# Order of sums and products in the gated output stage, and the first loads requested from two engines

## What is computed

```
s1, s2 = cond[:, :256], cond[:, 256:]
# attention layers (two): x*s1 is normalised over its channels; q, k, v, w and u are projections,
# each scaled by rsqrt(square(weight) . square(style) + 1e-8)
x = x + attention(x)
# scan layers (two):
xr, gate = split(x @ W_in.T)
xn = layernorm(silu(conv4(xr + t_emb)))            # 512 channels
h  = clip(h * ad + bd * xn_t, -10, 10)             # for each token, 16 states x 512 channels
ys = sum over states of c * h
y  = ys + D * xn
x  = x + (y * silu(gate)) @ W_out.T
```

## Time and profile before

| | |
|---|---|
| median of 3 runs | 1805.43 us (1805.3, 1805.43, 1807.08) |
| profiled execution, its own time | 1802.89 us |
| span of its trace | 1801.1 us |
| mean granted TensorE clock | 0.983 |
| busy: PE, DVE, ACT, POOL | 94%, 90%, 73%, 38% |
| moved by DMA | 226.85 MB |

### The profile page before, as it was taken

How to read it: one execution, slowest core, us unless ns; L and a number is a source line. 1 busy time by engine, 2 the same in 40 slices (tenths; PEclk the granted TensorE clock), 3 DMA queues, 4 the chain that set the end, 5 groups by cost and what they waited for, 6 DMA issues and landing times.

```text
span 1801.1 us, 43797 instructions
## 1 busy us (share of the span) xinstructions
PE 1684.4 (94%) x14852; PEld 749.3 (42%) x14852; DVE 1629.7 (90%) x2492; ACT 1306.5 (73%) x2213; POOL 686.3 (38%) x702
## 2 busy tenths in 40 slices
PE   6999999999999999899999999999998999999998
PEld 3555555555554555332222224445553322222244
DVE  5899999999987999989999998679999999999976
ACT  5655556465646999889999992069998999999910
POOL 0223233232331332457676650002335576756400
PEclk9999999999999999799999999999998999999999
DMA  4000001000002344554555667624345445456677
GB/s 161 2 2 0 1 2 31 2 1 0 2 1 83 133 162 156 183 168 140 182 154 188 218 187 220 212 83 173 132 176 187 152 141 183 151 189 198 188 232 262
DMA packets 126312, 226.85 MB, mean 126 GB/s; under 512 B 35604, under 2 KB 61204, under 8 KB 117268
## 3 DMA queue, kind: packets, MB, share of 16 engines
q1 hardware_dynamic: 126200, 225.35, 38.2%
HBM read 141.95 MB, written 83.36 MB: 125 GB/s over the span
## 4 chain that ended last, share of the span: by engine, by line
PE 24%; ACT 19%; DVE 15%; issue 7%; DMA 3%; POOL 1%; DVEq 1%; ACTq 0%; SPq 0%; POOLq 0%
ACT R L1058 17%; PE PS L1173 5%; PE PS L1505 5%; PE PS L1522 5%; DVE q L2080 4%; DMA sgp<-sg_d 3%; PE PS L1571 2%; DVE acc L1762 2%; DVE z L1920 2%; PE PS L1365 2%; PE PS L1340 1%; PE PS L1382 1%; DVE yf L2116 1%; DVE xp L1758 1%; DVE z L1891 1%
## 5 line engine op out<-in xcount | busy, mean ns | idle before, releaser
L1058 ACT ACTIVATE R<-q,Ast 128x512 f32<-128x512 f32 x1016 | 633.0, 708 | 35.2 <-DVE q L2080 33.0
L2080 DVE SCALAR_TENSOR_TENSOR q<-R,PS 128x512 f32<-128x512 f32 x1008 | 610.9, 684 | 9.4 <-PE PS L1505 5.1
L629 POOL TENSOR_TENSOR Uw<-Ub,rowmask 96x512 bf16<-96x512 bf16 x256 | 335.6, 1344 | 145.4 <-PE PS L1505 133.3
L1505 PE MATMUL PS<-xq,Uw 97*128 97x512 bf16 x1024 | 329.3, 394 | 42.4 <-DVE q L2080 34.5
L1522 PE MATMUL PS<-q,Wy 128*32 128x512 f32 x2016 | 282.0, 615 | 0.4 <-DVE q L2080 0.4
L1505 PEld LDWEIGHTS PS<-xq,Uw 97*128 97x128 bf16 x1024 | 85.0, 97 | 362.0 <-DVE q L2080 270.8
L1173 PE MATMUL PS<-X,Win 128*128 (+1 forms) x456 | 213.9, 607 | 0.1
L1074 PE MATMUL PS<-xn,Wl 128*128 128x512 f32 x384 | 186.6, 610 | 0.8 <-DVE xn L1644 0.7
L550 POOL TENSOR_TENSOR ex<-ex,rs 128x1024 f32<-128x1024 f32 x32 | 76.8, 2400 | 164.2 <-DVE rs L1667 164.2
L1762 DVE SCALAR_TENSOR_TENSOR acc<-xp,Wc,acc 128x512 f32<-128x512 f32 x192 | 134.7, 752 | 2.6 <-DVE eC L1884 0.2
L543 POOL TENSOR_TENSOR vsc<-vTd,vs_t 128x1024 f32<-128x1024 f32 x16 | 41.6, 2600 | 217.9 <-ACT vTd L768 217.9
(11 more groups left out here) (183 smaller groups left out, 2622.7 us busy)
## 6 DMA issues: line engine op xcount, KB each, us to landing
xq<-xpart_d SPq DMA_DIRECT2D x384, 192.0 KB
sg_d<-sg SPq DMA_DIRECT2D x16, 1024.0 KB, 5.3
xn_d<-z SPq DMA_DIRECT2D x16, 1024.0 KB, 3.9
y_d<-ys SPq DMA_DIRECT2D x64, 256.0 KB, 3.9
xnp<-xn_d SPq DMA_DIRECT2D x16, 1024.0 KB, 8.0
sgp<-sg_d SPq DMA_DIRECT2D x16, 1024.0 KB, 11.6
xpart_d<-xh SPq DMA_DIRECT2D x16, 512.0 KB, 2.9
xpart_d<-xmi SPq DMA_DIRECT2D x16, 512.0 KB, 3.7
```

Source lines behind the costliest of these rows:

```text
L629: pl.tensor_tensor(Uw[0:XROWS, h, w, :, :, :], Ub[0:XROWS, w, 0:N, ds(s0, CH)].rearrange("p n t -> p t n").unsqueeze(2).broadcast_to([XROW ...
L1058: act.activation((end if end and (h, t) == (1, CH - 1) else R)[:, w, :], q[:, t % 2, w, :], ACT.Relu, scale=Ast[:, h, w, t:t + 1], bias=CL ...
L1505: pe.matmul(PS[:, w, :], Uw[0:KROWS, h, w, t, :, :].rearrange("p b n -> p (b n)"), xq[0:KROWS, hb, w, s8 % XT, :], start=True, stop=True). ...
L2080: v.scalar_tensor_tensor(out=q[:, s8 % 2, w, :], in0=R[:, w, :], scalar=2 * CLIP, in1=PS[:, w, :], op0=ALU.min, op1=ALU.subtract).then_inc ...
```

## The change

In `gated`, the four sums yf of a group are written first, in one loop, and the four products yg behind them, in a second one. A wait is added ahead of the first sum of each group but the very first: all products yg of the group before must be written, since they read yf.

At the start, X's group 0 and the weights Wl[0] are no longer requested by SP but by ACT, ahead of its first table load: X's group 0, then q and k (512 KB) with a semaphore of their own, then v, w and u (768 KB). ACT's squaring of q and k waits for the new semaphore, the other waits for Wl[0] stay with the old one, which now counts v, w and u.

```diff
+        w_qk_in = sem("att_weights0_qk")
...
         def _(sp):
             sp.dma_start(cond[:, :, :], condT).then_inc(cond_in, 16)
-            sp.dma_start(X[:, 0, :, :], xT[:, 0]).then_inc(x_in[0], 16)
             sp.dma_start(masks[:, :], masks_d).then_inc(spr_in, 16)
             sp.dma_start(spread[:, :, :], spread_d).then_inc(spr_in, 16)
-            sp.dma_start(Wl[0][:, :, :, :], attw[0]).then_inc(w_in[0], 16)
             sp.dma_start(X[:, 1, :, :], xT[:, 1]).then_inc(x_in[1], 16)
...
+            act.dma_start(X[:, 0, :, :], xT[:, 0]).then_inc(x_in[0], 16)
+            act.dma_start(Wl[0][:, 0:2, :, :], attw[0][:, 0:2]).then_inc(w_qk_in, 16)
+            act.dma_start(Wl[0][:, 2:5, :, :], attw[0][:, 2:5]).then_inc(w_in[0], 16)
             logarithm_set()
...
             def weight_squares(l, ws=range(5)):
-                act.wait_ge(w_in[l], 16)
+                if l == 0 and ws == range(2):
+                    act.wait_ge(w_qk_in, 16)
+                else:
+                    act.wait_ge(w_in[l], 16)
...
                 def gated(g):
                     it, u = l * G + g, g % 2
                     v.wait_ge(po_in[u], (l * (G // 2) + g // 2) * 32 + 32)
+                    if it:
+                        v.wait_ge(yg_r, it * DC)
                     for m in range(DC):
                         v.wait_ge(po_mm, it * DC + m + 1)
                         v.scalar_tensor_tensor(out=yf[:, m, :], in0=xnp[:, u, m, :], scalar=Dsk[:, m, :], in1=PS[:, m, :],
                                                op0=ALU.mult, op1=ALU.add).then_inc(yf_r, 1)
+                    for m in range(DC):
                         v.wait_ge(yf_r, it * DC + m + 1 + DC)
                         v.tensor_tensor(yg[:, u, m, :], yf[:, m, :], sgp[:, u, m, :], ALU.mult).then_inc(yg_r, 1)
```

## The result

| | before | changed |
|---|---|---|
| median | 1805.3 us (5 runs, 1800.24 to 1807.08) | 1791.3 us (5 runs, 1790.33 to 1793.67) |
| profiled execution, span | 1802.89, 1801.1 us | 1792.12, 1790.3 us |

The ratio is 0.9931, 95% interval 0.9914 to 0.9948: by it the change is 12 us faster (14.0 by the medians), where 7.4 were forecast. 1791.3 lies under the range's lower end of 1795.8.

A forecast was written before the change was run, and what follows sets the result against it. Loads of xnp, sgp and y were taken to pace the gated stages' middle, PE their end, Wl's landing the start. Terms -2.5 - 3.2 - 1.7 = -7.4 us from 1805.43 gave 1798.0 us, range 1795.8 to 1802.3.

The forecast's parts named there:

- the level: Whole kernel: the median of the runs shown, 1805.43 us, was the start from which the 7.4 us were subtracted.
- the middle stage's: Gated stage of the first of the last two layers: group 6's product starts sooner, -2.5 us, bounds -0.5 and -2.7.
- Pace of DVE: Gated stages, each group: sums start every 0.66 us, products every 0.61; fourth sum ends at 2.72, last product at 5.16.
- PE's queue: Gated stages: turn_y(g+1) stands before outward(g) and waits for the fourth sum; outward starts at 3.37 us, 2.07 sooner.
- Landings move with the first request: Gated stages: DMA engines are full until group 6 has its loads, so all landings move 0.46 us sooner.
- last: Gated stage of the last layer: group 6's product starts 3.8 or 2.7 us sooner; the middle, -3.2 us, was taken.
- Start: First loads: q and k land sooner, so ACT squares them sooner; -1.7 us, between gains of 0 and 2.5.
- the row-by-row end of the estimate: First loads: if engines take a row from each queue in turn, q and k land at 7.4 us, gain 2.5.
- The loads only sharing the bandwidth: Rival 2, start: Wl's first part lands at 11.3 us as before, at most 0.46 gained; 1799.7 us, chance 0.18.
- The stages set by the loads alone: Rival 3, gated stages: loads, not PE, set the end, each stage gives only 0.5 us; 1802.7 us, chance 0.15.
- The clock, the slower rival: Rival 4, last two products: PE's gathered waits drop the clock, 13.9 us become up to 27.8; 1811.9 us, chance 0.05.

The follow-up runs named there:

- e2: The kernel before with only the first loads changed (three requests on ACT), sums in the old order: 1797.84 us against 1800.35, ratio 0.9986.
- e3: The kernel before once more, without any edit, for a second profiled execution: ratio 0.9997, runs from 1794.4 to 1803.52 us.
- e4: The kernel before with Wl[0] cut in two transfers (q and k, then v, w and u), all requested by SP: 1798.26 us, ratio 0.9987.
- e1: The kernel before with only the order of sums and products changed, first loads still with SP: 1794.95 us against 1800.35, ratio 0.9968.
- e5: The changed kernel measured a second time, unedited, beside the kernel before: 1794.64 us against 1800.57, ratio 0.9976.
- e8: The kernel before with the new order of sums and Wl[0] cut in two on SP's queue, no requests moved to ACT: 1793.66 us, ratio 0.9966.
- e11: The changed kernel measured a third time, unedited, beside the kernel before: 1792.84 us against 1800.21, ratio 0.9955.
- e6: The kernel before (old order) without the loads of xnp and sgp for groups 2 to 7, output differs: 1794.61 us, ratio 0.9969.
- e7: New order of sums and products, without the loads of xnp and sgp for groups 2 to 7, against the kernel before: 1792.07 us, ratio 0.9958.
- e10: New order and split on SP, each stage's first gate load (group 2) requested behind group 1's products, against the kernel before: 1803.53 us, ratio 1.0020.

## Why the prediction was right or wrong

The landings and stages of all profiles with the gate loads requested alike, from each timeline, in us from the stage's first sum:

| | old order: before, e2, e3, e4 | new order: changed, e1, e5, e8, e11 (third run) |
|---|---|---|
| group 6's first sum, middle | 55.21, 53.20, 53.69, 56.00 (mean 54.5) | 52.21, 52.72, 53.42, 51.80, 50.86 (52.2) |
| group 6's first sum, last | 54.67, 57.05, 53.91, 53.77 (54.9) | 54.91, 54.94, 55.88, 55.02, 55.15 (55.2) |
| stage, middle | 81.46, 79.93, 80.16, 82.25 (81.0) | 76.49, 77.48, 77.70, 76.08, 75.98 (76.7) |
| stage, last | 75.30, 76.54, 73.30, 73.15 (74.6) | 72.33, 73.16, 74.26, 72.59, 73.95 (73.3) |

- **The step that failed is the level.** "The median of the runs shown is 2.5 us above it, so the forecast is 1805.43 - 7.4 = **1798.0 us**": this took three runs as the level from which to subtract. 78 later ones put the kernel before at 1800.2, which makes 5.2 of the 6.7 us by which 1791.3 lies under the forecast; from 1800.2 the same 7.4 give 1792.8, itself under the range. Of its width only 0.6 us, from 1805.4 - 9.0 = 1796.4 down to 1795.8, was left for what runs differ by. In the first set the kernel before stood 5.1 us above its later level and the changed kernel 1.5 to 3.3 under its own; why is open. The difference forecast, 7.4 us or 0.9959, is 0.0005 from the mean of the three measurements, lies inside the interval of the third, 0.0002 below the second's and 0.0011 above the first's.
- **The term that was mis-sized is the middle stage's,** -2.5 forecast with a bound of -2.7, -4.97 in the pair of profiles and -4.2 by the means below. The order on PE's queue gives 1.96 of it (e6 and e7); the rest came with group 6's landing, counted as 0.46 us sooner and 2.3 sooner in the means.
- **Pace of DVE, right.** 2.72 and 2.49 us, groups 0 and 1 5.22 us apart instead of 5.54. The Trainium skill, "VectorE: DVE Perf Modes", section "The DRAIN you can't avoid", says that a semaphore after each operation of a chain costs nothing extra; the prediction read that for the wait too. Read so it does not fit: a product that waits for its own sum starts 0.78 us behind it, an independent sum 0.66. Of the semaphore alone no run here tells, since both orders have one after every operation.
- **PE's queue, right.** Where PE waited for the sums of the changed kernel, the product came 3.38 to 3.41 us behind the first of them, 3.37 forecast. Without loads the stage gains 1.96 and 1.97 of 2.07 forecast.
- **Landings move with the first request: borne out for a late request, off in size for the sooner one.** The request was 0.49 us sooner (5.22 instead of 5.71 behind the first sum, 0.46 forecast) and e10 shows that a late first request makes all later landings late. That the engines have no hole behind it was argued and is borne out in part (group 3 of e10). But in the means the middle stage's landing moved by -2.3 and the last's by +0.3. The terms: middle stage -2.5 forecast and -4.2 by the means (above), last -3.2 forecast and -1.3; together -5.7 and -5.5, and e1 measured 5.8. In the last stage half of the difference between -3.8 and -2.7 was counted as gained from "8.57 instead of 7.03"; no other profile of the old order has a fall of the clock there, and three of five of the new order have one (last point). Why the landings of the two stages differ is open.
- **Start, -1.7 forecast, 2.06 in the pair of profiles, 1.9 by the means, 2.5 by e2's ratio.** The size was right, the way partly wrong. q and k landed at 6.4 us, before the 7.4 of the row-by-row end of the estimate, and what held the start was spread, a small transfer of the other queue, by which ACT's mean part was 0.54 us late. The prediction had it "go up to 0.9 us sooner"; it was requested 0.47 us sooner and landed 2.1 us later than before (8.7 against 6.6).
- **Rivals.** The loads only sharing the bandwidth: out for q and k, though its reason, the same DMA engines behind both queues, fits spread's coming late. The stages set by the loads alone, 0.5 us each: out, the means give 4.2 and 1.3, and by e6 and e7 the order pays without the loads. e10 shows that the loads set the pace up to group 6, as the prediction assumed. The clock, the slower rival: its mechanism is real, its size small. Between 1760 and 1770 us the clock fell in e1, e5 and the third run of the changed kernel (0.83 over 10 us in each), not in the changed kernel's own profile and e8, nor in e2, e3 and e4; the product of group 6 then came 4.28, 4.44 and 4.86 us behind its first sum, where the changed kernel's own profile has 3.41 and e8 3.64. That is 0.6 to 1.5 us, and the last two products ran at full speed every time (13.9 us). All five profiles of the new order have the gathered wait there, 1.92 to 2.31 us long, and two of them kept the full clock behind it. Three of five against one of four does not show that the wait is the cause.

## What to carry to other kernels

Where a queue of one engine holds two kinds of waits in a fixed order, write first what the earlier wait wants: four sums before four products let PE go 2 us sooner, twice. In a stage that the loads fill, see that the first request is not late: 5.2 us there cost 9.7 us over two stages. Cut a transfer at what is wanted first before giving it a queue of its own. For terms of a few us in 1800, take the level and the stage lengths from several executions, and the level from more than one set: one profile gave a stage 2 us off its own repetition, and one set a level 5 us off four others. A version without the loads shows how long a stage is without them, and so what is left to win there.

## What the runs showed that I had not expected

Two queues do not share by order of request. With 1792 KB requested by ACT beside SP's queue, cond (128 KB, requested at the same time as before) took 4.0 us to land and spread 7.0, where SP alone had 2.1 and 4.5, while q and k with 512 KB, behind another 512 KB, took 5.2. The other profiles repeat it: 3.7 to 3.9 and 6.7 to 6.8 us with ACT's requests (e2, e5, third run of the changed kernel), 2.0 to 2.2 and 3.2 to 4.2 without (e1, e3, e4, e8). The landing of group 6 in the two stages, the same code on the same sizes, differs by 2.2 to 4.3 us in each of the five profiles of the new order, and by 0.3 in the mean of the old. Why is open.
